# Moving the columns' product and the turn of h1 in the tile loop of a recommendation tower

## The reference

```python
e = jnp.stack([tbl_0[ids[:, 0]], ..., tbl_26[ids[:, 26]]], axis=1)   # 2048 x 27 x 128
interactions = jnp.einsum('bfd,bgd->bfg', e, e)
flat = interactions[:, TRIU_I, TRIU_J]                               # 351 pairs
h = concatenate([e.reshape(2048, 27 * 128), flat, dense_ctx], axis=1)  # 3823 columns
h = maximum(h @ W_top1 + b_top1, 0)                                  # 512
h = maximum(h @ W_top2 + b_top2, 0)                                  # 256
y = h @ W_top3                                                       # 1
```

## Time and profile before

| | |
|---|---|
| median of 3 runs | 712.8 us (710.17 to 718.01) |
| profiled execution, its own time | 709.83 us |
| its span | 708.0 us |
| PE busy | 574.9 us, 81% |
| POOL busy | 416.2 us, 59% |
| DVE busy / ACT busy | 347.6 us / 232.3 us |
| mean granted clock of PE | 0.908 of 2.4 GHz |

### The profile page before, as it was taken

The page is one execution under the profiler, slowest core; times in us unless marked ns, Lnnn a source line. Parts: engine busy times, 40 slices in busy tenths (PEclk is TensorE's granted clock), DMA queues, the critical chain, the costliest instruction groups (busy, mean ns, idle before and its releaser), DMA issues.

```text
span 708.0 us, 7882 instructions
## 1 busy us (share of the span) xinstructions
PE 574.9 (81%) x2578; PEld 504.6 (71%) x2578; DVE 347.6 (49%) x1140; ACT 232.3 (33%) x703; POOL 416.2 (59%) x450
## 2 busy tenths in 40 slices
PE   2606688989889898959959896897968979698898
PEld 1505577868778787948848795786857868697786
DVE  4305462819264563808337281554707355372755
ACT  4204423324251513315232331514315161323441
POOL 6775565666666565665746667365664666556001
PEclk9956899989989998989989899799987999989999
DMA  6613411111111111111111111011110111111000
GB/s 211 217 52 110 131 45 44 46 46 44 45 45 50 41 49 41 48 45 39 47 29 50 44 42 52 27 49 42 46 52 26 49 41 49 42 41 46 12 1 1
DMA packets 19581, 37.84 MB, mean 53 GB/s; under 512 B 7780, under 2 KB 8804, under 8 KB 19540
## 3 DMA queue, kind: packets, MB, share of 16 engines
q0 software_dynamic: 13824, 28.34, 15.1%
q1 hardware_dynamic: 5716, 8.99, 4.0%
HBM read 37.30 MB, written 0.01 MB: 53 GB/s over the span
## 4 chain that ended last, share of the span: by engine, by line
PE 59%; another core or an unknown queue 20%; DVE 8%; issue 6%; ACT 5%; DMA 1%; SPq 0%; ACTq 0%; DVEq 0%
PE ps_acc L298 12%; PE ps_acc L299 11%; PE ps_acc L300 11%; PE ps_gram L323 10%; DVE g_buf L666 6%; PE ps_acc L356 6%; PE ps_t L269 5%; PE ps_gram L400 3%; ACT g_buf L582 2%; DVE emb_x L645 1%; DMA g_buf<-in_W_top 1%; ACT emb_x L534 1%; ACT h_t L571 1%; PE ps_gram L352 1%
## 5 line engine op out<-in xcount | busy, mean ns | idle before, releaser
L242 POOL DMA_INDIRECT emb<-in_tbl,idx x405 | 385.8, 953 | 233.4 <-issue 109.4
L298 PE MATMUL ps_acc<-w_hi,emb_x 128*128 128x512 f32 x432 | 211.1, 489 | 28.7 <-DVE emb_x L645 26.6
L645 DVE TENSOR_TENSOR emb_x<-ps_t,emb_x 128x512 fp32r<-128x512 f32 (+1 forms) x111 | 73.9, 667 | 249.6 <-ACT emb_x L534 165.2
L299 PE MATMUL ps_acc<-w_lo,emb_x 128*128 128x512 f32 x432 | 182.7, 423 | 0.0
L300 PE MATMUL ps_acc<-w_hi,emb_x 128*128 128x512 f32 x432 | 181.0, 419 | 0.0
L666 DVE COPY g_buf<-ps_gram 32x112 f32<-32x112 f32 x480 | 129.8, 270 | 93.6 <-PE ps_gram L323 63.1
L323 PE MATMUL ps_gram<-emb_x 128*128 128x224 f32 x480 | 99.5, 335 | 79.2 <-DVE emb_x L645 41.2
L298 PEld LDWEIGHTS ps_acc<-w_hi,emb_x 128*128 128x128 f32 x432 | 131.9, 305 | 35.3 <-DVE emb_x L645 28.0
L323 PEld LDWEIGHTS ps_gram<-emb_x 128*128 128x128 f32 x480 | 83.4, 231 | 102.0 <-DVE emb_x L645 45.1
L582 ACT ACTIVATE g_buf<-ps_gram 32x112 f32<-32x112 f32 x480 | 122.2, 255 | 99.0 <-PE ps_gram L323 64.8
L534 ACT ACTIVATE emb_x<-ps_t 128x512 fp32r<-128x512 f32 (+1 forms) x111 | 63.1, 583 | 272.7 <-PE ps_t L269 137.4
(11 more groups left out here) (61 smaller groups left out, 163.2 us busy)
## 6 DMA issues: line engine op xcount, KB each, us to landing
g_buf<-in_W_top SPq DMA_DIRECT2D x27, 256.0 KB
emb<-in_tbl,idx POOLq DMA_INDIRECT x405
w_cols<-in_W_top SPq DMA_DIRECT2D x1, 512.0 KB
w<-in_W_top SPq DMA_DIRECT2D x1, 512.0 KB
emb<-in_tbl,idx_first POOLq DMA_INDIRECT x27
w_cols<-in_W_top SPq DMA_DIRECT2D x1, 222.0 KB
idx<-in_ids SPq DMA_DIRECT2D x1, 216.0 KB, 4.9
ctx_rows<-in_dense_ctx SPq DMA_DIRECT2D x4, 32.0 KB
```

The source lines that it names most:

```text
L242: pool.indirect_dma_start(out=emb[:, f * D:(f + 1) * D], out_offset=None, in_=tables[f], in_offset=bass.IndirectOffsetOnAxis(ap=rows, axis ...
L298: pe.matmul(acc, emb_part(0, f), w_hi[:, f, :], start=(f == 0), stop=False)
L299: pe.matmul(acc, emb_part(0, f), w_lo[:, f, :], start=False, stop=False)
L645: dve.tensor_tensor(group_part(1, g), turned_bank(n, g), group_part(0, g).bitcast(fp32), ALU.subtract).then_inc(s_emb_lo, 1)
```

## The change

In tiles 1 to 14 the columns' product moves from behind turn 4 to behind turn 5, with two feature products on either side of turn 5. Turn 6 then comes after two more products, and behind it stand four products, the turn of h1 and a fifth product; then the gram stage begins, with four products between its units and no longer seven (the first two of those seven stood ahead of unit 0). Two products stay behind layer 2 as before. On ACT the relu and the taking of h1 move behind the split of group 6. In tile 0, which has no columns, the list `BEFORE_UNIT` alone changes: two products no longer stand ahead of unit 0, one fewer stands ahead of unit 3, and the three stand behind the gram stage. The last tile's list is untouched.

```diff
-            BEFORE_UNIT = [2, 0, 0, 2, 0, 0, 1, 0, 0, 1, 0, 0, 1, 0, 0, 0]
+            BEFORE_UNIT = [0, 0, 0, 1, 0, 0, 1, 0, 0, 1, 0, 0, 1, 0, 0, 0]
...
             for t in range(TILES - 1):
-                multiply_group(t, 0)
-                turn_group(t, 2)
-                multiply_group(t, 1)
-                turn_group(t, 3)
-                multiply_group(t, 2)
-                if t > 0:
+                todo = list(range(NF))
+                if t == 0:
+
+                    for g in range(2, NG):
+                        multiply_next(GF)
+                        turn_group(t, g)
+                else:
+
+                    multiply_next(GF)
+                    turn_group(t, 2)
+                    multiply_next(GF)
+                    turn_group(t, 3)
+                    multiply_next(GF)
                     turn_columns(t - 1)
-                turn_group(t, 4)
-                if t > 0:
+                    turn_group(t, 4)
+                    multiply_next(2)
+                    turn_group(t, 5)
                     multiply_columns(t - 1)
-                multiply_group(t, 3)
-                turn_group(t, 5)
-                if t > 0:
+                    multiply_next(2)
+                    turn_group(t, 6)
+                    multiply_next(4)
                     turn_h1(t - 1)
...
@@ scalar @@
-                    if t > 0 and g == 4:
+                    if t > 0 and g == 6:
                         relu_h1(t - 1)
-                    if t > 0 and g == 5:
                         take_h1(t - 1)
```

More of the change, by code:

```diff
@@ L437, in last_layer_2, with multiply_next @@
                 last.then_inc(s_l2, 1)
-            BEFORE_UNIT = [2, 0, 0, 2, 0, 0, 1, 0, 0, 1, 0, 0, 1, 0, 0, 0]
-            assert len(BEFORE_UNIT) == UNITS and sum(BEFORE_UNIT) <= NF - 4 * GF
+            BEFORE_UNIT = [0, 0, 0, 1, 0, 0, 1, 0, 0, 1, 0, 0, 1, 0, 0, 0]
+            assert len(BEFORE_UNIT) == UNITS
+            def multiply_next(count):
+                for _ in range(min(count, len(todo))):
+                    multiply(t, todo.pop(0))
             pe.wait_ge(s_ident, 1)
@@ L449, in _ @@
             for t in range(TILES - 1):
-                multiply_group(t, 0)
-                turn_group(t, 2)
-                multiply_group(t, 1)
-                turn_group(t, 3)
-                multiply_group(t, 2)
-                if t > 0:
+                todo = list(range(NF))
[9 more added lines that the diff above has]
+                    multiply_next(GF)
                     turn_columns(t - 1)
-                turn_group(t, 4)
-                if t > 0:
+                    turn_group(t, 4)
+                    multiply_next(2)
+                    turn_group(t, 5)
                     multiply_columns(t - 1)
-                multiply_group(t, 3)
-                turn_group(t, 5)
-                if t > 0:
+                    multiply_next(2)
+                    turn_group(t, 6)
+                    multiply_next(4)
                     turn_h1(t - 1)
[L464 to L468, removed]
+                    multiply_next(1)
                 for k in range(UNITS):
-                    for _ in range(min(BEFORE_UNIT[k], NF - f)):
-                        multiply(t, f)
-                        f += 1
+                    multiply_next(BEFORE_UNIT[k])
                     gram_unit(t, k)
@@ L477, in _ @@
                     layer_2(t - 1)
-                while f < NF:
-                    multiply(t, f)
-                    f += 1
+                multiply_next(len(todo))
             t = TILES - 1
             todo = list(range(NF))
-            def multiply_next(count):
-                for _ in range(count):
-                    multiply(t, todo.pop(0))
             turn_group(t, 2)
```

## The result

| | before | after |
|---|---|---|
| median | 714.1 us (710.17 to 718.01, 4 runs) | 758.4 us (752.53 to 763.25, 4 runs) |
| ratio | | 1.062, 95% interval 1.052 to 1.071 |
| profiled execution: own time, span | 709.83, 708.0 us | 763.25, 761.4 us |
| PE busy | 81% | 75% |
| mean granted clock | 0.908 | 0.874 |

The change costs 6.2%. ACT's lines are lower by two than before, DVE's by three; PE's are the same.

The account below looks back on a forecast made before the run. PE set the pace, idle before the first gram unit because its signals wait for POOL's pauses. 13 periods of 44.1 us (+37.5), tile 1 (+4.7) and tile 0 (+1) gave +43 on 709.8: 753 us, range 706 to 778.

Parts of the forecast that it names:

- Turn 5's signal before POOL ends group 4: Turn 5 ends some 4 us sooner, signal 0 to 2 us late, so POOL no longer pauses before group 5.
- Release of turn 6: ACT's split of group 6 starts at POOL's pause behind group 5, 30.3 us after L400, against 24.7 to 25.7.
- Turn of h1 and unit 0: After split and relu on ACT, PE's turn starts 31.5 us after L400, the first gram unit at 33.0.
- Gram stage: From gram unit 0 to L400: 11.1 us, tile 7's 12.2 less 1.1 for one product fewer.
- Period: One tile, L400 to L400: 33.0 + 11.1 = 44.1 us, against 41.2 on average before.
- second point: Turn 6's signal slips through, hold shifts to h1 and gram signals, POOL pauses behind group 6; period 44 to 45.
- Clock: Sign in the changed kernel's trace: PE's mean granted clock is not above 0.908.
- Rival A: Turn 6's signal comes promptly, the hole before unit 0 goes: 657 us, 640 to 700; chance 0.14.
- Rival B: Turn 5's signal held until POOL's check of group 5, release 24.7 us after L400: 706 to 722; chance 0.15.
- C: POOL's pauses too short, gram stage held up too, period 46.4: 785 us, half the tiles 770; above 778 chance 0.07.

Follow-up runs that it names:

- e11: The kernel before, with POOL pausing (four memsets) before group 5 and ACT's split of group 5 waiting for a mark behind that pause: 653.8 us, 1.132 of before.
- e12: The changed kernel, with POOL pausing (four memsets) before group 6 and ACT's split of group 6 waiting for the mark: 730.6 us, 1.265 of before.
- e10: The kernel before, unedited, traced on a chip of the experiments: 579.37 us.
- e1 to e4: No gathers behind tile 0: changed kernel 570.4, kernel before 577.7; changed kernel with POOL memsets instead 571.8, with SP's plain DMAs instead 570.9 us.

## Why the prediction was right

753 us was forecast, 758.4 measured. No step of the chain failed in the typical tile, but one sentence on the cause was too broad, and that the two times lie so close is in part luck. Between the two profiled executions the change is 53.4 us (763.25 - 709.83), where the sum had 43; between the medians of the result it is 44.3.

- **Turn 5's signal before POOL ends group 4.** Right. It came 2.1 us late in tile 14, where 0 to 2 was said, but up to 4.5 in others and 7.2 in tile 3: that range was too narrow, and it did no harm because POOL comes to group 5 only 22.8 us after L400. POOL paused there in no tile (0.58 us in tile 3 was the most); it had paused in ten.
- **Release of turn 6.** Forecast 30.3 us after L400, measured 30.6. The release followed POOL's end by 3.05 us and not by 2.3 to 2.6; POOL started group 2 at 7.8 us and not 7.6.
- **Turn of h1 and unit 0.** Forecast 31.5 and 33.0 us after L400, measured 31.7 and 33.9. From the turn to unit 0 it took 2.2 us (706.26 - 704.07) and not 1.5. Both ran wholly at half clock (granted 0.50 from 704.07 to 708.30; the turn 1.11 us where it takes 0.60 at full), while I had 0.4 for the turn and a product mostly at half clock. This is the term that was most mis-sized in a typical tile.
- **Gram stage.** Forecast 11.1, measured 10.5, 1.7 under tile 7's 12.2 where I took off 1.1. The missing product alone is worth 0.9 between the tiles shown of e11 and e12, and 0.6 on average over their 13. The likely rest, not tested: part of the half-clock stretch now lies ahead of unit 0, so that the two misses belong together (0.7 too short and 0.6 too long).
- **Period.** Forecast 44.1, measured 44.3 to 44.8 in nine of 13. The other four are near the prediction's "second point" (a signal slips through and the hold falls on h1), for which 44 to 45 was said; only in tile 5 did turn 6's signal slip through, in the others it came after a short pause or none. They took 45.5 to 46.8, and add about 7 us. The 13 periods came to 49 us more than before (716.77 - 132.07 = 584.7 against 535.75) where 37.5 was forecast. The tiles ahead of them came to 132.07 - 127.71 = 4.4 more, where 5.7 was. The profiled run of after, 763.25, is the longest of its four, 53 us above the profiled run of before.
- **Clock.** Not above 0.908, as said: 0.874.
- **Rival A** speaks of a machine that exists: that of the experiments. Its condition holds there (0.03 us in e10), and its gain does not come (ratio 1.003), since the hole of 3 us that it was to fill is itself a product of late signals. The sentence of the Trainium skill on the semaphore tail, "TensorE: Matmul & The Clock Gate", section "The cost: per-tile semaphore tail" (0.06 us for one increment, an estimate from that page), agrees with e10 (0.03 us) and disagrees with the traces of the result (2.1 and 10.6 us).
- **Rival B** did not occur in any tile, nor did C over the whole (tiles 9 and 10, with pauses of 1.0 and 1.1 us before group 6, are of its kind).

The sentence that was too broad is "PE's signals are held back while POOL issues gathers in a long row". e10 has the longest row of all and holds nothing. What the runs show is narrower: in the traces of the result the release mostly keeps to POOL's pauses (not in tile 6 of the changed kernel), in the experiments there is no hold. That a signal let through only at POOL's pause produces these tiles, and that moving the pause from group 5 to group 6 costs 5 us a tile, is shown by e11 and e12, on another machine than the result's. What holds the signals, and why only there, stays open; no experiment could be made under the hold itself. Since the kernels without gathers (e1 to e4) ran where there is no hold in any case, it isn't shown that the gathers are its cause and not only its companion.

## What to carry to other kernels

Where a wait names a signal that was raised long ago, measure from the raising instruction's end to the waiter's start, and look which third engine's pause the start keeps to; a better-looking order upstream can then move the release to a later pause. A delay that one machine shows can be imposed by hand on another: a mark behind a pause costs two kernels, and gave the price of the move (5.2 to 5.5 us a tile). Count its periods and not only its total, since a mark costs most in the first tile. And before a schedule is tuned against such holes, run the unchanged kernel again on another chip: here its 3 us holes came with the machine.

## What was not expected of the hardware

- One kernel, unchanged, took 712.8 us when the result was measured and 577.5, 576.8 and 577.8 us on the three chips of the experiments. POOL's busy time was the same within 0.5 us in the two traces (416.2 and 416.7), the gathers started 1.25 us apart in both; but turn 5's signal came 4.7 us late in one and 0.03 us in the other, and the granted clock was 0.908 against 0.991.
- The two traces are 130 us apart (708.0 and 577.6): 36 us arise before tile 1's layer 2, 94.5 in the 13 periods behind it. A split that waits for a program's own pause, in each of 15 tiles, brought back 27 and 47 of them (e11). The rest is not shown.
